# Layer 3's table on four 32-row tiles of TensorE, products on two 64-row tiles, and a new order ahead of the loop

## The reference

```
x = x + conv1d(x, w0, 9 taps, 4 groups) + (cond @ c_weight.T)[:, :, None] + bias
for n in 1, 2, 3:
    h   = gelu(gelu(cond @ W0 + b0) @ W1 + b1)
    att = softmax(h @ W2 + b2)                       # 8 weights per sample
    x   = x + einsum("boi,bih->boh", att @ weight_n, x) + (att @ bias_k)[:, :, None]
```

## Time and profile before

| | |
|---|---|
| median of three runs | 324.08 us (323.95 to 324.44) |
| profiled execution, own time | 325.95 us |
| its span | 324.1 us |
| PE busy | 314.7 us, 97% of the span |
| DVE, ACT, POOL busy | 264.2, 228.0, 129.0 us |
| DMA | 104.80 MB, mean 323 GB/s |
| longest waits of PE | 2.2 us for mixrow, 1.1 and 1.0 us for DVE, 0.4 us each for mix_lo and a_dup |

### The profile page before, as it was taken

The page is one execution under the profiler, slowest core; times in us unless marked ns, Lnnn a source line. Parts: engine busy times, 40 slices in busy tenths (PEclk is TensorE's granted clock), DMA queues, the critical chain, the costliest instruction groups (busy, mean ns, idle before and its releaser), DMA issues.

```text
span 324.1 us, 6093 instructions
## 1 busy us (share of the span) xinstructions
PE 314.7 (97%) x1482; PEld 257.6 (79%) x1482; DVE 264.2 (82%) x292; ACT 228.0 (70%) x345; POOL 129.0 (40%) x269
## 2 busy tenths in 40 slices
PE   8879999999999999999999999999999999999994
PEld 8767968888888888888888888888888888888883
DVE  4575778879887888888988799888888898899784
ACT  5343686777788777767777788776777777787564
POOL 8001088843444344443344434545433333333400
PEclk9999999999999999999999999999999999999999
DMA  7993437899899999999998999899999999997687
GB/s 216 281 287 152 163 117 260 325 355 351 326 359 342 370 347 381 356 352 379 338 371 321 365 342 378 327 369 347 360 357 345 385 340 358 346 363 286 266 356 291
DMA packets 30381, 104.80 MB, mean 323 GB/s; under 512 B 3402, under 2 KB 3658, under 8 KB 22539
## 3 DMA queue, kind: packets, MB, share of 16 engines
q1 hardware_dynamic: 30372, 104.70, 87.8%
HBM read 36.53 MB, written 33.55 MB: 216 GB/s over the span
## 4 chain that ended last, share of the span: by engine, by line
PE 88%; DMA 4%; DVE 2%; POOL 2%; ACT 1%; SPq 1%; issue 1%; POOLq 0%
PE bank L399 54%; PE bank L441 9%; PE bank L443 9%; PE bank L442 9%; PE bank L407 4%; DMA early<-in_mixrow 4%; PE bank L520 1%; POOL table L334 1%; POOL a_dup L364 1%; DVE x_lo L740 1%; ACT x_hi L607 1%; PE bank L496 1%; DVE table L832 1%; DVE early L787 0%; SPq L270 0%
## 5 line engine op out<-in xcount | busy, mean ns | idle before, releaser
L614 ACT ACTIVATE conv_sb<-bank 128x512 f32<-128x512 f32 x128 | 76.3, 596 | 64.9 <-PE bank L399 60.9
L354 POOL COPY a_diag<-table 64x64 f32 (+1 forms) x128 | 50.6, 396 | 144.9 <-PE bank L407 110.3
L740 DVE TENSOR_TENSOR x_lo<-x_sb,x_hi 128x2064 fp32r<-128x2064 f32 x32 | 73.9, 2308 | 20.7 <-ACT x_hi L607 19.3
L399 PE MATMUL bank<-x_hi,toep_hi 128*128 128x512 f32 x256 | 84.5, 412 | 0.0
L364 POOL COPY a_dup<-table 64x128 f32 (+1 forms) x128 | 71.6, 560 | 30.9 <-DVE table L832 13.3
L399 PE MATMUL bank<-x_lo,toep_hi 128*128 128x512 f32 x256 | 80.7, 396 | 0.0
L399 PE MATMUL bank<-x_hi,toep_lo 128*128 128x512 f32 x256 | 80.5, 395 | 0.0
L757 DVE TENSOR_TENSOR ybuf<-ybuf 128x1024 fp32r<-128x1024 f32 x62 | 77.0, 1244 | 2.7 <-ACT ybuf L618 1.6
L634 ACT ACTIVATE out_sb<-bank,beta 128x512 f32<-128x512 f32 x93 | 63.4, 684 | 4.8 <-DMA out<-out_sb 1.5
L607 ACT ACTIVATE x_hi<-x_sb 128x2064 fp32r<-128x2064 f32 x32 | 61.7, 1928 | 5.4 <-DMA x_sb<-in_x 5.4
L399 PEld LDWEIGHTS bank<-x_hi,toep_lo 128*128 128x128 f32 x256 | 48.3, 189 | 12.0
(11 more groups left out here) (92 smaller groups left out, 175.7 us busy)
## 6 DMA issues: line engine op xcount, KB each, us to landing
x_sb<-in_x SPq DMA_DIRECT2D x32, 1032.0 KB, 7.9
ybuf<-conv_sb SPq DMA_DIRECT2D x128, 256.0 KB, 4.9
out<-out_sb SPq DMA_DIRECT2D x29, 1024.0 KB, 7.6
out<-out_sb SPq DMA_DIRECT2D x8, 256.0 KB, 2.0
out_sb<-conv_sb SPq DMA_DIRECT2D x4, 256.0 KB
out<-x_sb SPq DMA_DIRECT2D x4, 256.0 KB, 2.8
early<-in_pairs SPq DMA_DIRECT2D x1, 640.0 KB, 6.2
x_sb<-in_toep SPq DMA_DIRECT2D x1, 640.0 KB, 8.0
```

The costliest lines, as they stand in the source:

```text
L354: nc.gpsimd.tensor_copy(a3_diag[rows, par, :, C * h + NH * e:C * h + NH * e + NH], table[0][C * e:C * e + C, here, h, :]).then_inc(comp_in, 1)
L399: last = mm(o, w[:, d, g, :], v[:, par, g, :, d:d + J], start=i + d == 0, stop=i + d == 3)
L614: nc.scalar.activation(conv_sb[:, par, g, :], conv_ps[g % banks][:, :], ACT.Copy).then_inc(conv_out, 1)
L740: nc.vector.tensor_tensor(x_lo[:, par].rearrange("p g s j -> p (g s j)"), x_sb[:, par].rearrange("p g s j -> p (g s j)"), x_hi[:, par].rea ...
```

## The change

The changed kernel computes the same. What differs:

- **Layer 3's table.** `mrow[0]` is cut into four column blocks of 1024, each held with its 9 rows in a group of 32 partitions of its own (`mrow[0][32*i:32*i+9]`, four DMAs of 36 KB in place of one of 144 KB; POOL clears 1024 columns instead of 4096). `coef` holds layer 3's coefficients once per group. `tables3(r)` issues 16 products of 32 rows x 128 columns, four row groups in turn, each into its own bank; r = 0, 1 give the eight parts. The number of products stays 32.
- **Pair products.** `pair1` and `pair2` no longer hold zeros: four products of 64 rows and 512 columns, two row groups in turn, instead of eight of 128 rows and 256 columns. The `pairs` input falls from 640 KB to 384 KB. The copies to `mrow[1]` are eight DMAs of 128 KB in pieces of 1 KB, before four of 256 KB in pieces of 2 KB; one bank is copied by DVE and three by ACT, before two each.
- **Bias early.** The `c0` products stand before the logits, in bank 5, and DVE copies them before the softmax.
- **Taps on POOL.** `taps` and `toep_lo` move from DVE to POOL.
- **Order.** `mixrow` is loaded before the own rows of layers 2 and 1. `conv(0)` stands as one block before `bias_turn(0)`; tables 8 to 15 are issued in three runs around `bias_products(1)` and `bias_turn(1)`. ACT's `x_high(1)` moves up before `vcol_copy(0)`, `x_high(2)` before table 14. DVE's `x_low(0)` is cut in group 0 and the rest, `bias_sum(1)` comes after `x_low(1)`. Three blank products stand behind `tables3`.

The core of the diff:

```diff
@@ SP
-            sp.dma_start(mrow[0][0:RS * K + 1:RS], own_h[0:K + 1]).then_inc(rows3_in, 16)
+            for i in range(RT):
+                n = C * C // RT
+                sp.dma_start(mrow[0][32 * i:32 * i + K + 1], own_h[0:K + 1, n * i:n * i + n]).then_inc(rows3_in, 16)
             load(0, 0)
+            sp.dma_start(mixrow, mixrow_h).then_inc(mixrow_in, 16)
             sp.wait_ge(rows21_zero, 1)
...
-            sp.dma_start(mixrow, mixrow_h).then_inc(mixrow_in, 16)
-            for l in range(LQ):
-                sp.dma_start(mrow[1][pair_row(l)::2 * RS].rearrange("m (a n) -> m a n", a=CB),
+            sp.wait_ge(pprod_act, 3)
+            sp.wait_ge(pprod_dve, 1)
+            for l in range(K):
+                sp.dma_start(mrow[1][l:l + RS * (K - 1) + 1:RS].rearrange("m (a n) -> m a n", a=CB),
                              prod[:, l].rearrange("p c k -> p (c k)")).then_inc(rows21_in, 16)
             sp.wait_ge(toep_lo_set, 1)
             load(1, 1)
@@ POOL
+            pool.wait_ge(toep_in, 16)
+            nc.gpsimd.tensor_tensor(taps, taps, eyes.to_broadcast([128, 2, G, 128]), ALU.add).then_inc(toep_set, 1)
+            pool.wait_ge(toep_hi_set, 1)
+            nc.gpsimd.tensor_tensor(toep_lo[:].rearrange("p d g m -> p (d g m)"), toep,
+                                    toep_hi[:].rearrange("p d g m -> p (d g m)").bitcast(F32),
+                                    ALU.subtract).then_inc(toep_lo_set, 1)
@@ PE
+            def pair_products(c):
+                for t in range(2):
+                    rows = slice(C * t, C * t + C)
+                    mm(prod_bank[2 * t + c][:, :], pair1[rows, c, :], pair2[rows, :], start=True, stop=True).then_inc(pprod_ps, 1)
+            def tables3(r):
+                for j in range(NG):
+                    for i in range(RT):
+                        rows = slice(32 * i, 32 * i + 32)
+                        at = 2 * C * (NG * r + j)
+                        last = mm(bank[BANKS[RT * r + i]][:, B * j:B * j + B], mrow[0][rows, at:at + 2 * C],
+                                  coef_t[rows, 0, :], start=True, stop=True)
+                        if j == NG - 1:
+                            last.then_inc(tab_ps, 1)
...
+            tables3(0)
+            pe.wait_ge(coef_t_set, 2)
+            pe.wait_ge(pprod_act, 3)
+            pe.wait_ge(pprod_dve, 1)
+            tables3(1)
+            taken(BANKS.index(1))
+            stream(3, 1)
             bias_products(0)
...
+            taken(BANKS.index(0))
             conv(0, 0, 0, banks=2)
+            taken(BANKS.index(1))
+            pe.wait_ge(xlo_set, 1)
+            for g in range(1, G):
+                conv(0, 0, g, banks=2)
             bias_turn(0)
+            for t in (8, 9, 10):
+                tables(t)
             bias_products(1)
+            for t in (11, 12, 13):
+                tables(t)
             bias_turn(1)
-            tables(8)
+            tables(14)
+            tables(15)
             bias_products(2)
@@ DVE
+            dve.wait_ge(c0_ps, 2)
+            nc.vector.tensor_copy(vrow[:], bank[5][:, 0:C]).then_inc(c0_set, 1)
...
             table_bank(1)
             table_bank(3)
             table_bank(5)
+            dve.wait_ge(xhi_set, 1)
+            for g, done in ((slice(0, 1), xlo_first), (slice(1, G), xlo_set)):
+                nc.vector.tensor_tensor(x_lo[:, 0, g], x_sb[:, 0, g], x_hi[:, 0, g].bitcast(F32),
+                                        ALU.subtract).then_inc(done, 1)
+            table_bank(7)
             bias_sum(0)
             x_low(1, 1)
             table_bank(9)
+            bias_sum(1)
+            table_bank(11)
+            table_bank(13)
+            table_bank(15)
             bias_sum(2)
```

More of the change, by code:

```diff
@@ L50 @@
 NTAB = NT * TG
+PARTS = (0, 2, 4, 6, 1, 3, 5, 7) + tuple(range(TG))
+BANKS = (4, 1, 2, 0, 7, 5, 6, 3, 4, 6, 7, 2, 3, 4, 6, 7)
 ACT_TAKES = (0, 2, 4, 6, 8, 10, 12, 14)
-RS = 4
-OWN = 2
-CB = 8
-RUN = C * C // CB
-LQ = K // 2
-def pair_row(l):
-    return l // 2 + RS * (l % 2)
+RT = 4
+RS = 12
+OWN = K
+EYE = OWN + 2
+CB = 16
 NET = dict(cond=B, w0=NL * D, b01=2 * NL, cw=C, fcol=1, w1=NL * D, w2=NL * K)
 FIRST = NET["cond"] + NET["w0"] + NET["b01"]
-EARLY = dict(net=sum(NET.values()), mixrow=NL * K * C, pair1=CB * 128, pair2=LQ * C, vadd=C)
+EARLY = dict(net=sum(NET.values()), mixrow=NL * K * C, pair1=2 * 128, pair2=K * C, vadd=C)
 ROW = dict(frow=C, b2=NL * K)
@@ L443, in mix, with stream @@
                 mm(o, m_hi, v_lo, start=False, stop=True).then_inc(mix_done, 1)
-            def stream(n):
+            def stream(n, b):
                 for _ in range(n):
-                    mm(bank[0][:, 0:128], blank[:], blank[:], start=True, stop=True)
+                    mm(bank[b][:, 0:128], blank[:], blank[:], start=True, stop=True)
             pe.wait_ge(blank_set, 1)
-            stream(5)
+            stream(5, 0)
             pe.wait_ge(net0_in, 16)
@@ L477, in _ @@
                    stop=n == NL - 1).then_inc(logit_ps, 1)
[L478 to L480 removed]
+            pe.wait_ge(pairs_in, 16)
+            pe.wait_ge(hid1_set, NL)
+            pair_products(0)
+            pe.wait_ge(c0_set, 2)
+            pair_products(1)
             pe.wait_ge(kept_in, 16)
             pe.wait_ge(coef_zero, 3)
[L484 removed]
+            pe.wait_ge(coef_set, 3)
             for t in range(NT):
@@ L513, in tables @@
+            def tables(t):
                 if t == TG:
-                    pe.wait_ge(rows21_in, 16 * (LQ + 2))
-                if t >= TB:
-                    wait(pe, tab_act, act_banks(t - TB + 1))
-                    wait(pe, tab_dve, dve_banks(t - TB + 1))
+                    pe.wait_ge(rows21_in, 16 * (K + 3))
+                taken(max(u for u in range(t) if BANKS[u] == BANKS[t]))
                 for i in range(NG):
-                    at = 2 * C * (NG * c + i)
-                    last = mm(t_bank[t % TB][:, B * i:B * i + B], mrow[n][:, at:at + 2 * C], coef_t[:, n, :],
+                    at = 2 * C * (NG * PARTS[t] + i)
+                    last = mm(bank[BANKS[t]][:, B * i:B * i + B], mrow[1][:, at:at + 2 * C], coef_t[:, 1, :],
@@ L799, in _ @@
             nc.vector.memset(mrow[1], 0.0).then_inc(rows21_zero, 1)
+            dve.wait_ge(c0_ps, 2)
+            nc.vector.tensor_copy(vrow[:], bank[5][:, 0:C]).then_inc(c0_set, 1)
+            dve.wait_ge(ones_set, 2)
+            nc.vector.tensor_scalar(vcol[0:C, :], bank[5][0:C, B:2 * B], fcol, None, ALU.add).then_inc(c0_set, 1)
             logits = bank[4][:, 0:NL * K].rearrange("b (n k) -> b n k", n=NL)
@@ L964 @@
     }
-    pairs = np.zeros((2, C, CB * 128 + LQ * C), f)
-    for e in range(2):
-        first = pairs[e, :, 0:CB * 128].reshape(C, RS, 2, 2, K, CB)
-        first[:, :, :, e] = ws[0][:, :, at].reshape(K, C, 2, CB, RS).transpose(1, 4, 2, 0, 3)
-        pairs[e, :, CB * 128:] = ws[1][LQ * e:LQ * e + LQ].transpose(2, 0, 1).reshape(C, LQ * C)
+    pairs = np.zeros((2, C, 2 * 128 + K * C), f)
+    cols = ws[0][:, :, at].reshape(K, C, 2, CB, 2)
+    for t in range(2):
+        pairs[t, :, 0:2 * 128] = cols[..., t].transpose(1, 2, 0, 3).reshape(C, 2 * 128)
+        pairs[t, :, 2 * 128:] = ws[1].transpose(2, 0, 1).reshape(C, K * C)
     pairs = pairs.reshape(128, -1)
```

159 lines of the change are left out of this document (56 added, 103 removed).

## The result

| | before | changed |
|---|---|---|
| median, us | 324.01 (322.83 to 327.42, 20 runs) | 322.13 (321.17 to 325.90, 20 runs) |
| ratio | | 0.9946, 95% interval 0.9920 to 0.9971 |
| profiled execution, own time and span | 325.95, 324.1 | 323.18, 321.3 |

The changed kernel is 0.54% faster: 1.9 us between the medians, where 5.2 were forecast; 322.13 lies above the range (317.2 to 321.9). The direction was right and the size was not.

The account below looks back on a forecast made before the run. Time was taken as PE's entry into the conv-mix alternation plus a constant; the chain through x of quad 1, ending on DVE, moved the first mix from 48.77 to 43.6, 5.2 us earlier: 324.08 to 318.9 us, range 317.2 to 321.9.

Parts of the forecast that it names:

- x of quad 1: Input load before the first mix: claimed on the path, landing at 25.6 us (25.0 to 29.7), against 26.2 before.
- 1.2 less for the pairs ... I take +0.6: Landing of x of quad 1: 1.2 us gained by the smaller pairs block, 0.6 us lost to eight smaller-piece copies.
- counted as costing nothing: Start-up: the early c0 products, six passes, would run while PE waits for the second gelu, at no cost.
- The queue before it is full: DMA queue ahead of x of quad 1: claimed full at share 0.95, so the load's issue time would not count.
- Out of the loop nothing should come back: Steady loop after the first mix: PE's share leaves no gap, so the start-up gain of 5.2 us would stay.
- 34.8 and a copy of 0.69: Chain to the first mix: tables 14 and 15 end at 34.8, then the copy of part 15 ends at 35.7.
- tiles side by side: Layer 3's table and pair products: 1.8 and 1.9 us if overlapping; rival without overlap: gain 4.3 us, chance 0.13.
- the library's reload: POOL, before the taps: some 6 us from 4.7, ending at 10.7 and leaving the sum as it is.
- the chain behind it: From x of quad 1 landing at 25.6 through ACT, DVE and PE steps to the first mix at 43.6 us.
- The first conv: PE's start-up: conv(0) would start at 18.6 instead of 24.82, after mixrow's landing at 17.9 and bias product 0.
- the clock: Rival: PE idle from about 13 to 17.9 us lowers its clock; gain 3.8 us, chance 0.10.
- Small pieces cost by number: Rival on the product copies: x of quad 1 lands at 28 to 29.7, gain 2.8 to 1.1 us, chance 0.12.

Follow-up runs that it names:

- before_again: The kernel before, unchanged, profiled once more: own time 323.98 us.
- pool_waits_prod: Changed kernel with POOL's taps waiting for the coefficients and DVE copying the fourth product bank ahead of them: 322.71 us, ratio 0.9930 to the kernel before.
- half_bytes: Changed kernel with its eight product-row copies at half their bytes, leaving work out: 320.24 us, ratio 0.9866 to the kernel before.
- mixed: Changed kernel with pair products, rows and four sixteen-row copies as in the kernel before: 321.95 us, ratio 0.9914 to the kernel before.
- after_again: The changed kernel, unchanged, measured and profiled once more: 322.41 us, ratio 0.9956 to the kernel before.
- prod_first: Changed kernel with DVE copying the fourth product bank before the first coefficients, measured twice: 321.05 and 322.66 us, ratios 0.9896 and 0.9923 to the kernel before.
- pool_waits: Changed kernel with POOL's taps waiting until DVE has written the coefficients: 323.16 us, ratio 0.9953 to the kernel before.
- ij: Changed kernel with the two loops around layer 3's 32 table products exchanged, so neighbours share rows: ratio 0.9921 to the kernel before.
- x2_late: Changed kernel with quad 2's x load held until quad 1's x lands: 322.85 us, 0.9956; also with DVE's fourth product bank copied first: 321.66 us, 0.9915.
- before_16rows: Kernel before with each of four product-row copies cut into two column halves, sixteen rows and 1 KB pieces: 324.43 us, ratio 0.9987 to the kernel before.
- mixed_prod: mixed with DVE's copy of the fourth product bank ahead of its coefficient copy: 321.40 us, ratio 0.9898 to the kernel before.
- x1_early: Changed kernel with the load of x for quad 1 issued after two of eight product copies: 327.56 us, ratio 1.0094 to the kernel before.

## Why the prediction was wrong

- **x of quad 1: 2.6 us.** The step that failed is its landing: "1.2 less for the pairs ... I take +0.6", which is 0.6 us earlier than in the kernel before. At executions near the median it landed at 24.2 in the kernel before (before_again) and at about 26.1 in the changed one: that is 1.9 us later. (The 26.1 is an estimate: the median of 322.13, less the 277.9 us from the first mix to the end, less the 18.1 from the landing to the first mix; the two profiles have 26.95 at 323.18 us and 25.86 at 321.57.) The first mix is 46.8 and 44.2 there, 2.6 us earlier and not 5.2. In the sum this term was mis-sized by 2.5 us.
- **That 25.6 was nearly met was luck.** It was worked out from 26.2, the landing in a profile whose DMAs were 2.0 us late. I had noted that this execution was 1.9 us above the median and treated the difference as a constant at the ends; the two profiles of before show that it lies in the first 25 us, in just the stretch that the change replaces. The error in the base hid the error in the step.
- **The reasons that I gave for 25.6.** The copies could not be issued from 11.4, but from 13.11. `att` was held 1.24 us by POOL; the softmax starts at 8.50 instead of 7.62, since the `c0` products, which I had counted as costing nothing, stand ahead of the logits; and DVE's last product copy stood behind the transposes. But pool_waits_prod issued them from 10.82 and x landed no earlier, so this isn't what counted. "The queue before it is full" is not so either: eight rows keep eight engines busy. I had priced the copies by bytes and by pieces, and not by their rows. That the rows are the cause isn't shown for the changed kernel: with sixteen of them x landed at 26.5 and 27.5. Why it lands late there stays open; fewer bytes help (half_bytes), an earlier issue does not.
- **The end: 0.7 us.** "Out of the loop nothing should come back". From the first mix to the end of the execution it is 277.2 us in both profiles of before (325.95 - 48.77, 323.98 - 46.79) and 278.0 and 277.8 in those of the changed kernel, whose last stores take 3.4 us for 2.8. In mixed it is 277.2 again (321.94 - 44.69), so this part comes with the smaller `pairs` block or what goes with it. I had counted that block's 256 KB as a gain of 1.2 us and nothing else.
- Together 5.2 - 2.6 - 0.7 = 1.9, the measured difference.
- A slip in the sum: 34.8 and a copy of 0.69 are 35.5, not 35.7. It changes the rest by 0.2 us.

Right were: tiles side by side (2.07 us against 1.8, pair products 1.99 against 1.9); POOL 2.35 against 2.3; no cost of the library's reload that shows; `a_dup` no longer meets `x_lo` (four copies in 1.34 us); x of quad 1 as the transfer that the first mix follows; and the chain behind it. Forecast were 43.6 - 25.6 = 18.0 us from landing to first mix. Measured were 18.3 in the changed kernel, and 17.9, 18.3, 18.3, 17.9, 17.9, 17.9, 18.3 and 18.3 in after_again, both of prod_first, pool_waits, pool_waits_prod, ij and both of x2_late. The first conv at 16.96 instead of 18.6 follows mixrow, which landed at 15.6 instead of 17.9 (in after_again at 14.7, with the conv at 18.00); I had no reason for that, and it gained nothing.

Of the rivals, the clock did fall, to its level of 1.2 GHz (0.50) for 3.4 us: from 30.43 in the changed kernel's profile, from 12.91 in after_again, after PE had stood 2.9 us in two waits and 1.8 us in one. The table passes that fell in it are 0.21 us apart, 0.11 on either side, as the prediction had priced it. The profiles with 18.3 us are those in which it stood at 0.50 somewhere between 28 and 34, the ones with 17.9 had it at 1.00 there: 0.4 us. Ahead of the landing a fall costs nothing that shows. "Small pieces cost by number" is not what was seen: before_16rows has the pieces of 1 KB and x at 24.7, in the kernel before.

Open: what would bring x of quad 1 forward. Only half_bytes was clearly faster than the changed kernel (its interval ends at 0.9904), and it leaves half of the rows out. And why the last stores depend on `pairs`: where the buffers lie in the device's memory would be a guess. No version clearly beats the changed kernel; mixed_prod (0.9898) and prod_first (0.9896, then 0.9923) are the nearest, with intervals that overlap its 0.9920 to 0.9971.

## What to carry to other kernels

A landing of a DMA in a start-up is one draw: two profiles of one kernel had the same landings 2 us apart here. Take the landings before and after each from more than one profile before you forecast a difference of that size, and when a number comes true, ask whether its base did: 25.6 was nearly met while the step behind it was wrong by 2.5 us. Price a DMA by the rows of its slowest dimension as well as by bytes and pieces. Where several transfers share a start-up, count what all of them need together: x of quad 1 ahead of the product rows made these late (x1_early), copies on sixteen engines went with a late mixrow (mixed). Work moved to POOL can hold a tiny DVE operation on the path for almost its whole length (2.18 of 2.35 us).

## What the runs showed of the hardware that I had not expected

- A DVE product of two SBUF inputs, 24 columns, took 0.18 us alone and 1.42, 1.90 and 2.18 us while POOL ran its two-input add of 2.35 us; in x2_late a DVE copy of 16 columns stood 2.33 us in the same way. The earlier trace rows show the reverse, POOL standing for DVE.
- Eight destination rows: at the most 8.3 to 8.8 pieces in flight whether SP alone or SP and ACT issue, whether the pieces are 1 or 2 KB.
- 64 passes of 32 rows and 128 columns: 2.07 us in alternating row groups, 5.00 us with four products at a time in one group; 128 rows need 0.112 each, 7.2 us for 64.
- The last four stores of the kernel, 256 KB each, land in 2.8 us where an input has 640 KB and in 3.4 where it has 384, in all of 20 profiles.
- The landing of x of quad 1 did not follow its issue: 16.06 to 27.26, 17.43 to 27.99, 17.44 to 24.67, 18.66 to 25.86, 20.55 (with half the copies) to 25.54.
- A full DMA share is not a full rate: 225 GB/s at a share of 1.00 in mixed, 224 at 0.76 in the changed kernel, 281 at 0.95 in before_again, all from 14 to 24 us.
